# A gated recurrent block on one core: the last sequence's end in two halves, a run-up of 50 transpositions, and a new order on every engine

## The reference

```
xn  = layernorm(x)                            # over the 128 features, no affine part
rkv = xn @ W_rkv + b_rkv                      # 128 x 384, split in r, k, v
r, k = sigmoid(r), exp(k);  kv = k * v
y   = scan(y[t] = lam * y[t-1] + u[t])        # over time, for u = kv and for u = k, lam per unit
s   = ((scan(kv) + gamma * kv) / (scan(k) + gamma * k + 1e-6) * r) @ W_o + b_o
g   = silu(mx(xn) @ mx(W_f).T + b_f)          # mx: FP6 values on blocks of 32 with one scale each
out = x + s * g
```

## Time and profile before

| | us |
|---|---|
| median of 3 runs | 120.75 (120.02 to 122.67) |
| profiled execution | 120.27 |
| its span, first to last instruction | 118.5 |
| PE busy | 109.9 (93%) |
| DVE busy | 107.1 (90%) |
| ACT busy | 102.0 (86%) |
| POOL busy | 100.6 (85%) |
| mean granted clock of PE | 0.986 of full speed |

### The profile page before, as it was taken

One profiled execution on the slowest core, in us unless ns is written; L12 is line 12 of the kernel. 1 busy time (PEld: TensorE's weight loads), 2 busy tenths in 40 slices (PEclk: granted clock), 3 DMA queues, 4 the chain that ended last, 5 costly groups with the idle time before them and its releaser, 6 DMA issues.

```text
span 118.5 us, 1729 instructions
## 1 busy us (share of the span) xinstructions
PE 109.9 (93%) x407; PEld 61.1 (52%) x407; DVE 107.1 (90%) x173; ACT 102.0 (86%) x184; POOL 100.6 (85%) x136
## 2 busy tenths in 40 slices
PE   4958999779999999999999999999999999999970
PEld 4945444345456455564564545555556455464450
DVE  0547999999999999999999999999999999998881
ACT  4048599999999999999999999999899999799800
POOL 2289689967999998999998999999999999899600
PEclk9996799999999999999999999999999999999999
DMA  3879950000000201020002020111120211202027
GB/s 70 236 228 401 390 203 0 0 0 3 6 6 0 89 19 69 0 89 0 0 6 89 0 89 0 45 44 55 39 97 0 89 45 44 89 0 89 0 89 266
DMA packets 6025, 8.82 MB, mean 74 GB/s; under 512 B 1536, under 2 KB 1920, under 8 KB 6016
## 3 DMA queue, kind: packets, MB, share of 16 engines
q1 hardware_dynamic: 5040, 8.72, 20.5%
q10 hardware_dynamic: 976, 0.00, 0.4%
HBM read 4.53 MB, written 4.19 MB: 74 GB/s over the span
## 4 chain that ended last, share of the span: by engine, by line
PE 73%; DVE 8%; DMA 6%; POOL 3%; SPq 3%; ACT 2%; issue 2%; DVEq 1%; POOLq 0%
PE taken_ps L1004 30%; PE turned_ps L983 10%; PE so_ps L1060 10%; PE v_ps L1032 9%; PE num_ps L1046 7%; DMA x_all<-in_L_attn_inputs_dram 6%; PE so_ps L1066 5%; DVE stats L458 2%; POOL q L312 2%; PE turned_ps L1060 1%; SPq L233 1%; DVE own_ps L467 1%; DVE x_all L531 1%; ACT xn L744 1%; DVE num_ps L505 1%
## 5 line engine op out<-in xcount | busy, mean ns | idle before, releaser
L1004 PE MATMUL taken_ps<-xnT,wrkv_sb 128*128 128x512 f32 x64 | 33.1, 614 | 0.6 <-ACT xnT L753 0.6
L744 ACT ACTIVATE xn<-x_all,shift,rstd 128x128 f32<-128x128 f32 x48 | 20.1, 489 | 5.6 <-POOL shift L293 5.6
L341 POOL TENSOR_TENSOR mixed<-mixed,den 128x512 f32<-128x512 f32 x16 | 20.6, 1285 | 1.0 <-DVE mixed L520 0.5
L335 POOL TENSOR_TENSOR den<-den,gk 128x512 f32<-128x512 f32 x16 | 20.4, 1285 | 0.7 <-DVE den L496 0.6
L505 DVE TENSOR_TENSOR_SCAN num_ps<-own_ps,kv 128x512 f32<-128x512 f32 x16 | 19.3, 1208 | 0.1
L496 DVE TENSOR_TENSOR_SCAN den<-own_ps,k 128x512 f32<-128x512 f32 x16 | 19.2, 1206 | 0.0
L727 ACT ACT_TABLE_LOAD x14 | 18.0, 1283 | 0.9 <-PEq L1229 0.7
L458 DVE BATCH_NORM_STATS2 stats<-x_all 128x6 f32<-128x256 f32 x32 | 11.8, 418 | 6.3 <-DMA x_all<-in_L_attn_inputs_dram 6.3
L319 POOL TENSOR_TENSOR xd<-q,scale 128x512 f32<-128x512 fp8e4 x16 | 16.9, 1057 | 0.0
L312 POOL TENSOR_TENSOR q<-xn,inv_scale 128x512 fp8e4<-128x512 f32 x16 | 16.9, 1056 | 0.0
L1004 PE MATMUL taken_ps<-xdT,wdT 128*128 128x512 f32 x32 | 16.6, 599 | 0.0
(11 more groups left out here) (71 smaller groups left out, 191.5 us busy)
## 6 DMA issues: line engine op xcount, KB each, us to landing
x_all<-in_L_attn_inputs_dram SPq DMA_DIRECT2D x16, 256.0 KB, 6.7
out_dram<-x_all SPq DMA_DIRECT2D x16, 256.0 KB, 2.0
wrkv_sb<-in_L_attn_W_rkv_dram SPq DMA_DIRECT2D x1, 192.0 KB, 4.1
wf_sb<-in_L_ffn_weight_dram SPq DMA_DIRECT2D x1, 64.0 KB, 6.7
wo_sb<-in_L_attn_W_o_dram SPq DMA_DIRECT2D x1, 64.0 KB, 6.5
cols<-in_L_attn_nu_log_dram ACTq DMA_DIRECT2D x1, 0.5 KB, 3.7
cols<-in_L_attn_gamma_log_dram ACTq DMA_DIRECT2D x1, 0.5 KB, 4.1
cols<-in_L_attn_b_o_dram ACTq DMA_DIRECT2D x1, 0.5 KB, 4.3
```

What stands on the lines that cost most here:

```text
L335: nc.gpsimd.tensor_tensor(den[:, n % DEN, :], den[:, n % DEN, :], gk[:, n % KS, :], ALU.add)\
L341: nc.gpsimd.tensor_tensor(mixed[:, n % MIX, :], mixed[:, n % MIX, :], den[:, n % DEN, :], ALU.mult)\
L744: ins = nc.scalar.activation(xn[:, n % XN, j * D:(j + 1) * D], x_all[:, n, j * D:(j + 1) * D], ACT.Identity, bias=shift[:, t:t + 1], scale ...
L1004: nc.tensor.matmul(taken_ps[i % 2][:, :], weights, moving, start=True, stop=True).then_inc(filled, 1)
```

## The change

Three things change.

1. `WARM_UP` goes from 32 to 50.
2. The end of sequence 15 goes in two halves of 256 steps. The first half's ratio stays on POOL, the second half's is on DVE (`late_ratio`). Each half then has its own projection, gating, turning back, residual and store. The first half uses the bank `v_ps`, the second `taken_ps[0]`.
3. The lists of calls of PE, DVE, ACT and POOL, `TURNS` and `TAKEN` are in another order from the fourth or so call on. Number and kind of the other instructions stay as they are (14 table loads, the same six `gamma_kv` on DVE).

The helpers also take an argument m for several sequences at once, `FIRST` is 0, `result_ready` is called `dve_result`: none of these changes an instruction, since m is 1 in every call. `scan_num(0)` waits for the decay column too, since it now stands ahead of `scan_den(0)`.

```diff
-    WARM_UP = 32
+    WARM_UP = 50
     TURNS = [
-        ("xn", 0), ("xn", 1), ("xn", 2), ("xn", 3), ("xd", 0), ("xn", 4), ("xd", 1), ("xn", 5), ("xn", 6),
+        ("xn", 0), ("xn", 1), ("xn", 2), ("xn", 3), ("xn", 4), ("xn", 5), ("xd", 0), ("xd", 1), ("xd", 2),
...
+        late_mixed = sb("late_mixed", [P, 2, 2 * P])
+        late_gated = sb("late_gated", [P, 2, 2 * P])
+        LAST = SEQS - 1
+        LATE_BANKS = [v_ps, taken_ps[0]]
+        def pairs(ap):
+            return ap.rearrange("f (p j) -> f p j", j=2)
+        def half(ap, h):
+            return in_time(ap)[:, :, 2 * h:2 * h + 2]
...
-            for n in range(SEQS):
-                sp.wait_ge(result_ready, n + 1)
+            for n in STORES:
+                if n == LAST:
+                    for h in range(2):
+                        sp.wait_ge(late_result, h + 1)
+                        sp.dma_start(out_v[:, n, h * 2 * D:(h + 1) * 2 * D], x_all[:, n, h * 2 * D:(h + 1) * 2 * D])\
+                            .then_inc(stored, 16)
+                    break
+                sp.wait_ge(dve_result, n + 1)
                 sp.dma_start(out_v[:, n, :], x_all[:, n, :]).then_inc(stored, 16)
...
+            def late_ratio():
+                pool.wait_ge(inv_ready, SEQS)
+                pool.wait_ge(numr_ready, SEQS)
+                nc.gpsimd.tensor_tensor(pairs(late_mixed[:, 0, :]), half(mixed[:, LAST % MIX, :], 0),
+                                        half(den[:, LAST % DEN, :], 0), ALU.mult).then_inc(late_ratio_pool, 1)
...
+            def late_ratio():
+                dve.wait_ge(inv_ready, SEQS)
+                dve.wait_ge(numr_ready, SEQS)
+                nc.vector.tensor_tensor(pairs(late_mixed[:, 1, :]), half(mixed[:, LAST % MIX, :], 1),
+                                        half(den[:, LAST % DEN, :], 1), ALU.mult).then_inc(late_ratio_dve, 1)
+            def late_gating(h):
+                dve.wait_ge(taken_used, taken("z", LAST) + 1)
+                dve.wait_ge(late_s, h + 1)
+                nc.vector.scalar_tensor_tensor(pairs(late_gated[:, h, :]), pairs(LATE_BANKS[h][:, 0:2 * P]), b_oc,
+                                               half(gate[:, LAST % GAT, :], h), ALU.add, ALU.mult)\
+                    .then_inc(late_gated_ready, 1)
+            def late_residual(h):
+                dve.wait_ge(late_o, h + 1)
+                nc.vector.tensor_tensor(x_all[:, LAST, h * 2 * D:(h + 1) * 2 * D], LATE_BANKS[h][:, 0:2 * D],
+                                        x_all[:, LAST, h * 2 * D:(h + 1) * 2 * D], ALU.add).then_inc(late_result, 1)
...
+            def late_project(h):
+                if h == 0:
+                    pe.wait_ge(kv_ready, SEQS)
+                    pe.wait_ge(late_ratio_pool, 1)
+                else:
+                    pe.wait_ge(taken_used, len(TAKEN))
+                    pe.wait_ge(late_ratio_dve, 1)
+                nc.tensor.matmul(LATE_BANKS[h][:, 0:2 * P], wos_sb[:, :], late_mixed[:, h, :], start=True, stop=True)\
+                    .then_inc(late_s, 1)
+            def late_untranspose(h):
+                pe.wait_ge(late_gated_ready, h + 1)
+                for j in range(2):
+                    ins = nc.tensor.transpose(LATE_BANKS[h][:, j * D:(j + 1) * D], pairs(late_gated[:, h, :])[:, :, j],
+                                              ident[:, :])
+                ins.then_inc(late_o, 1)
```

More of the change, by code:

```diff
@@ L431, in _ @@
-            ratio(9)
-            denominator(11)
+            quantise(12)
+            dequantise(11)
+            dequantise(12)
+            gamma_k(11)
+            gamma_k(12)
+            denominator(10)
+            denominator(11)
+            ratio(9)
+            quantise(13)
+            quantise(14)
+            dequantise(13)
+            gamma_k(13)
+            ratio(10)
+            dequantise(14)
             denominator(12)
-            dequantise(13)
-            ratio(10)
+            quantise(15)
@@ L585, in _ @@
             inverse_scales(0)
+            statistics(8)
+            statistics(9)
             block_maxima(1)
@@ L616, in _ @@
+            gating(0)
             key_values(4)
-            gating(0)
+            gamma_kv(2)
+            residual(0)
+            receive(2)
+            scan_den(3)
+            block_maxima(4)
             scan_num(3)
-            scan_den(3)
-            residual(0)
-            block_maxima(4)
-            receive(3)
+            statistics(13)
             gating(1)
-            scan_num(4)
-            residual(1)
-            statistics(12)
-            key_values(5)
-            receive(4)
@@ L629, in _ @@
             block_scales(4)
             inverse_scales(4)
+            scan_den(4)
+            receive(3)
+            residual(1)
+            key_values(5)
+            scan_num(4)
+            statistics(14)
+            statistics(15)
+            key_values(6)
+            receive(4)
+            scan_den(5)
+            key_values(7)
+            block_maxima(5)
+            gating(2)
             scan_num(5)
-            gating(2)
+            block_scales(5)
+            inverse_scales(5)
@@ L667, in _ @@
[L667 to L678 removed]
+            gamma_kv(7)
+            residual(4)
+            receive(7)
+            block_maxima(7)
+            scan_num(8)
+            scan_den(8)
+            gating(5)
+            key_values(10)
@@ L679, in _ @@
+            receive(8)
             block_scales(7)
             inverse_scales(7)
+            residual(5)
+            scan_den(9)
+            scan_num(9)
+            gating(6)
+            key_values(11)
+            gamma_kv(9)
+            residual(6)
+            scan_den(10)
+            receive(9)
+            gating(7)
+            scan_num(10)
+            scan_den(11)
+            residual(7)
+            block_maxima(8)
+            receive(10)
+            gating(8)
             scan_num(11)
-            gating(7)
@@ L700, in _ @@
+            receive(11)
+            scan_den(12)
+            key_values(13)
+            residual(9)
+            scan_num(12)
+            scan_den(13)
+            scan_den(14)
+            receive(12)
+            gating(10)
+            scan_num(13)
+            residual(10)
             gamma_kv(13)
@@ L835, in _ @@
             normalise(2)
+            keys(1)
             rough_std(3)
-            keys(1)
             normalise(3)
@@ L1150, in _ @@
-            ffn(6)
-            receptance(10)
-            gamma_kv(8)
+            untranspose(2)
+            ffn(3)
+            transpose_xd(6)
+            ffn(4)
+            transpose_xd(7)
+            project(3)
+            values(9)
+            receptance(7)
+            untranspose(3)
+            gamma_kv(6)
+            ffn(5)
+            ffn(6)
+            transpose_xd(8)
+            transpose_xn(10)
+            receptance(8)
+            project(4)
+            ffn(7)
+            transpose_xn(11)
@@ L1164, in _ @@
             project(6)
-            keys(13)
+            receptance(10)
+            ffn(8)
+            untranspose(6)
             transpose_xd(10)
-            gamma_kv(10)
-            untranspose(6)
-            ffn(8)
             values(12)
             project(7)
+            receptance(11)
+            transpose_xn(14)
             ffn(9)
+            untranspose(7)
+            gamma_kv(10)
+            keys(13)
+            project(8)
+            transpose_xn(15)
+            keys(14)
```

689 lines of the change are left out of this document (318 added, 371 removed), and 14 rows, old and new, of tables (TAKEN, TURNS).

## The result

The changed kernel takes 121.42 us (median of 7, 121.22 to 121.60) against 120.75: 1.0081 times as long, with an interval of 1.0051 to 1.0110. Some executions of any kernel run in a slower state of the chip; the medians contain them, the ratios and their intervals leave them out. So the change is a little slower, by about 1 us, where 119.7 was forecast. The profiled execution took 121.22 us with a span of 119.4, beside 120.27 and 118.5 before.

A forecast was written before the change was run, and what follows sets the result against it. DVE and PE were taken to be full at once, with room only at DVE's ends. Front and middle 0, tail 0.5 and store 0.2, taken as 0.6 in all: 120.27 - 0.6 = 119.7 us, range 118.8 to 121.5.

The forecast's parts named there:

- is a fixed list with almost no hole in it: DVE before the last sequence's numerator scan at 107.33: no reordering makes its list shorter; only its two ends have room.
- so it reaches 107.33 again if it waits for nothing: DVE in the middle: its list holds the same instructions, so the last numerator scan starts at 107.33 as before.
- runs from 23.45 to 25.4: The weights' quantisation on DVE in front, walked in the new order; PE stands from about 24.1 to 25.7.
- The middle, charged at 0: Hand-overs between PE and DVE: projections end 1 to 1.5 us ahead, up to 0.8 us waiting on PE's side; 0 charged.
- The rival that hand-overs eat the gain: DVE waits in the middle or halves cost a whole: 0.6 to 1.4 us, giving 120.3 to 121.1; chance 0.22.
- the range went up that far for waits on PE: Slower rival: PE waits at some 22 places, sequences 1 to 12, exceed its 0.8 us reserve, giving 123.3; chance 0.12.
- The first numerator scan was walked to 20.05: DVE in front: statistics, maxima, gamma and the first key-value product come first, so the front gain ends in DVE's queue.
- the count behind it: PE in front: 17 products done before the first projection at 31.65, 31.79 before, so PE neither wins nor loses.
- The run-up: Eighteen more transpositions on PE fill the hole before 9.4 us and keep the clock up; 0 us taken at the end.
- The rival's 1.7 us: Front gain reaches the end: the fast clock's 1.7 us go through, giving 118.0; chance 0.07.
- The tail: After the last scan: halving costs DVE 0.52, the 0.72 wait goes, a 0.66 wait comes; DVE ends 0.5 us earlier.
- The store: Last store, half as large, issued just behind the 15th sequence's: 0.2 us taken off its 2.6, bounds 0 and 0.6.

The follow-up runs named there:

- a_warm32: The changed kernel with a run-up of 32 instead of 50 transpositions: 121.26 us, ratio 1.0052 to the kernel before.
- b_psum: The kernel before with only the two scale columns of the weights' quantisation in PSUM instead of SBUF: 119.04 us, ratio 0.9900.
- b_warm50: The kernel before with only the run-up raised to 50 transpositions: 121.48 us, ratio 1.0061.
- b_half: The kernel before, old order up to the last scan, with sequence 15 ended in halves and stores issued in order of readiness: 120.54 us, ratio 1.0012.
- a_psum: The changed kernel with the two scale columns of the weights' quantisation in PSUM instead of SBUF: 119.96 us, ratio 0.9959 to the kernel before.
- a_outw: The changed kernel with out_weights moved on DVE to behind the decay column, where POOL is idle: 121.05 us, ratio 1.0030 to the kernel before.
- b_psum50: The kernel before with the weights' scale columns in PSUM and a run-up of 50: 119.68 us, ratio 0.9947.
- a_store: The changed kernel with SP's last stores issued in the order in which they are ready: 121.10 us, ratio 1.0042 to the kernel before.

## Why the prediction was wrong, and where it was right

**The step that failed:** what DVE does before the last scan "is a fixed list with almost no hole in it", and "so it reaches 107.33 again if it waits for nothing". It reached 108.49. The list is the same; its durations are not, since they depend on what POOL runs at that moment. The 1.16 us, from the two traces: loads that came earlier −0.30 (statistics of the fifth sequence at 10.37 instead of 10.68), `gam_diag` −0.24 (0.36 instead of 0.60; before, it ended just behind POOL's `q`), `out_weights` +0.62, the weights +0.77, and more idle time from 50 to 106 +0.31 (0.11 and 0.20). The sum is +1.16. So the terms that were mis-sized are the weights' quantisation ("runs from 23.45 to 25.4", the 1.95 of before; it took 2.72) and `out_weights` (0.21 taken over from before; it took 0.83). The evidence lay in the trace of before, in the two rows of `wq` and `wd`: one size, one kind, 0.88 and 0.29 us. An unexplained factor of three between like rows should have been asked about.

**The middle, charged at 0,** cost 0.31 more idle time than before, 0.22 of it one wait for PE before the `receive` at 98.74. The rival that hand-overs eat the gain was right in kind, but at half its lowest price. Most of the loss is the mechanism that no rival named. That 121.42 lies inside the stated range, at its upper edge, is luck: the range went up that far for waits on PE.

**The front.** The first numerator scan was walked to 20.05 and starts at 20.05. That is partly chance: −0.30, −0.24 and +0.62 nearly cancel. The weights began at 23.38 (walked 23.45) and ended at 26.10 (walked 25.4), and PE stood 1.87 us for them where 1.6 was walked. The first projection starts at 31.73 in the chain, close to the 31.65 walked and the 31.79 of before. But the count behind it is wrong: by then PE had done 16 products, not 17, since the new list has the first `ffn` product behind that projection. So PE did not come out even in front; it was 0.80 us behind (one product, 0.86, less 0.06). By a_warm32 PE had about 0.7 in reserve, so little of this can have reached the end, and none beyond the 0.31 of idle time on DVE.

**The run-up.** As forecast the clock stayed up: from 10 to 13 us the granted mean is 1.00, where the earlier trace rows had 0.50, and in the new order 50 against 32 transpositions bring nothing that the times show (a_warm32). The rival's 1.7 us is refuted. But the fall is a matter of the execution: with the same 32 transpositions a_warm32 has none there. Of the executions of the kernel before that enter the ratios of the experiments, the 29 with a mean clock of 0.986 or less have a median of 120.61 us, the 31 with 0.995 or more 120.26. This, and DVE's wait in b_psum, speak for some 0.35 us at the end in the old order, where 0 was taken. It is not shown: where the clock fell is known for the profiled executions alone, and b_warm50, which should have won it, was slower. (The rise near 6.2 is read from the spacing of the transpositions; the granted clock in the earlier trace rows is 1.00 from 1.5 us on.)

**The tail.** 8.05 us were forecast from the scan to DVE's end, 8.10 came. The half gatings and residuals are as forecast: from start to start 0.39 and 0.33, where 0.38 and 0.34 were taken (with the bounds of 0.30 and 0.60 a piece the halving costs 0.24 to 1.74, not 0.35 to 1.8). The half ratio on DVE differs: it takes 0.75 us, because POOL works on the other half until 112.62; in b_half, with POOL idle, it takes 0.42. It costs nothing, since DVE would have stood for the projection of sequence 14 anyway: that wait is 0.30 instead of the 0.66 forecast. The halves pay only together with the second gating ahead of `receive`.

**The store.** I took 0.2 off the 2.6 us; it became 2.85. SP issues in the order of the program, and the first half's store stood behind one that becomes ready 0.6 us later. The landing after issue is 2.0 us for a half as for a whole one, so a half-sized store is not quicker (the page after, part 6):

```profile
out_dram<-x_all SPq DMA_DIRECT2D x2, 128.0 KB, 2.0
```

**In sum:** forecast −0.6; the scan 1.16 late, tail −0.45, store +0.24, which gives +0.95 in the span (118.49 to 119.44). Mechanism and size are shown for the weights (a_psum, by the times too) and for `out_weights` (a_outw, by the trace). Not settled are the times of b_warm50 and b_psum50, and what the clock's fall in front costs in each order.

## What to carry to other kernels

Before taking over durations from an earlier trace, look for like instructions with unlike durations on DVE, and hold their ends against the ends of POOL's: a busy row can be a hidden wait. In this kernel a small TENSOR_TENSOR or TENSOR_SCALAR on DVE with all its operands in SBUF cost as much as the rest of the POOL instruction it met, at times of the next one too; moving one small operand to PSUM, or the instruction to a moment when POOL is idle, took that away. Stores belong in the queue in the order in which their data become ready, and a tail in halves paid here only together with work moved ahead to cover the wait for the product. Two engines can be full at once; then count what each has done at a common point of its list, as the 16 and 17 products here.

## What the runs showed of the hardware that was not expected

- A DVE instruction on 128 x 4 elements took 0.17 us with its output in PSUM (a_psum), 0.31 and 0.46 across the end of one POOL instruction, and 1.32 across two. Statistics, scans out of PSUM and reciprocals of the same stretches keep their durations (a reciprocal of 128 x 4: 0.18 in every kernel with SBUF columns), and so did a TENSOR_SCALAR on 128 x 1 (0.15 inside POOL's `q`).
- At the same place the price differs from execution to execution: `wscale`, started 0.29 to 0.30 us ahead of the end of POOL's `den`, took 0.31 us in the kernel before and 1.32 in b_warm50 and b_half.
- Moving one instruction out of a collision changes what the next ones meet (a_outw: 0.61 won at `wos_sb`, `wd` from 0.67 to 1.23, `wq` from 1.09 to 0.88, `wscale` from 0.46 to 0.18).
- PE stood for `wd` in the profiled execution of a_warm32 too, and there the clock fell afterwards (PE by stretch: us, busy, granted clock, DMA share, GB/s):

```profile
24.30:26.20 1.90, 0.03 (x1) 1.00 0.00 0
27.40:30.60 3.20, 3.20 (x8) 0.50 0.00 0
30.80:33.00 2.20, 2.20 (x7) 1.00 0.01 4
```

PE was busy through the whole stretch at the lower level (1.2 GHz). In the profiled execution of the changed kernel it stood as long, 1.87 us, and the clock stayed at the upper one. In that of a_store, with a run-up of 50, it stood 2.00 us and the granted mean was 0.50 from 28 to 31. What tells these executions apart is not shown.
